# Row groups of the TensorE array for the target products of two layers of a graph network

## The chip, the cores and the metric

One core of one Trainium2 chip. The metric is the device time of one execution in microseconds, as a median over runs. TensorE is PE in the profile (its weight loads PEld), VectorE is DVE, ScalarE is ACT, GpSimd is POOL, and SP is the engine that issues most DMAs.

## What is computed

Four graph layers on 6250 nodes of 128 features and 100000 edges (`src`, `dst`, edge attributes, types and weights). Every layer sums something of the edges into nodes, goes through small dense layers and normalisations, and is added to x:

```
edge_index = jnp.stack([src, dst])
x = _layernorm(x + _L0_gnn_ref(x, edge_attr_128, ...))  # segment_sum(edge_attr, src) / count, then 3 x (linear, relu, batch norm)
x = _layernorm(x + _L1_gnn_ref(x, edge_index, ...))     # segment_sum(x[src], dst) / degree, + x, linear, relu
x = _layernorm(x + _L2_gnn_ref(x, edge_index, edge_type_3, ...))  # messages by edge type, segment_sum to dst, linear, norm, gelu
x = _layernorm(x + _L3_gnn_ref(x, edge_index, edge_weight, ...))  # segment_sum(x[src] * norm, dst), linear, relu, batch norm
```

The change concerns the sums into nodes of the first layer (layer 0: edge attributes by `src`) and of the last one (layer 3: weighted messages by `dst`).

## The kernel before, in words

Nodes are 49 groups of 128 (`GROUPS`). A first part (up to about 1110 us) sorts the edges into blocks of 4 (`BLK`) by groups of source and target node, and writes them as rows to the tables `slots` and `gbuf` in HBM. From then on everything goes by tiles: a tile is 128 blocks of 4 edges, 258 tiles (`TILES`) in 43 rounds (`RR`) of 6 (`RING`).

Each layer q has a target stage, `reduce(q)`, which sums the rows of a tile into a group of nodes. The same name stands once in PE's program and once in DVE's. For tile t, at place r = 0 to 5 of its round:

- SP loads the tile's rows, 128 partitions by 4 edges of 128 features and a few more values, into place r of a ring (`load_wide` for layers 0 and 1, with a second ring for the odd rounds; `load_tiles`, line 618 on, for layers 2 and 3, where the load waits until the products of the tile that held the place are made).
- A one-hot of the 4 x 128 target lanes is made in `hots[:, r, :]`: by DVE in one instruction (`one_hot`, line 1831), or for the places in `SCALAR_HOTS` by ACT in five (lines 936 and 940). ACT has place 5 in layer 0 and places 2 and 5 in layer 3, so DVE makes 5 and 4 one-hots a round. They are made for the round after: `one_hot(i + 1, r)` stands right behind the add of tile (i, r).
- PE (line 1379) waits for the one-hot, the rows, and the add of the tile three before, and makes 4 f32 products, one-hot by rows, which add up in PSUM bank r % 3. A product contracts over all 128 block rows and gives 128 nodes by `width` columns (129 in layer 0, 128 in layer 3). Each f32 product is two LDWEIGHTS and two MATMULs, here called two passes. The last one counts `products` up.
- DVE (line 1841) waits for `products` and for its own add before (`added`), and adds the bank to `sums` at a column that a register gives. The registers of a round's six tiles are loaded at the round's start by `loaded(at_sum, ...)` (line 501). `added` begins at 3.

In the code:

```
pe.wait_ge(added, t + (q * TILES + 1))
wait_rows(pe, q, i if h is None else h, r, odd)
for j in range(BLK):
    ins = pe.matmul(bank(r % 3, width), hots[:, r, j * P:(j + 1) * P], rows[:, j, 0:width],
                    start=j == 0, stop=j == BLK - 1)
ins.then_inc(products, 1)
```

POOL (`keep_lanes`) and ACT (`keep_pays`) take values out of the rows in layer 0. In layers 0 and 3 no other engine uses PSUM during the target stage; in layer 2 other products run beside it in banks 4 to 6. What comes after each target stage waits for its end.

Of the kernel before, what the change touches and what calls it, by code (L numbers as in the profile page):

```python
# [5 lines left out]
ALU = mybir.AluOpType  # L6
# [10 lines left out]
P = 128  # L17
# [30 lines left out]
BLK = 4  # L48
# [4 lines left out]
TILES = 258  # L53
RING = 6
# [24 lines left out]
RESTS = 5  # L79
PAIRS = 3  # L80
MSG_BANKS = 4
MIXED = 4 * STEP
GATHERED = {1: 0, 2: TILES, 3: 2 * TILES}

# [13 lines left out]
def fills_before(stage, r):  # L98
    def of(s):
        if s[0] == "g":  # L100
            return EVEN if s[1] < 2 else RR
        if s[1] == 2:
            return RR if r % LANE_SETS == 0 else 0
        return (EVEN, ODD, 0)[r % LANE_SETS]

    return sum(of(s) for s in FILLS[:FILLS.index(stage)])
# [74 lines left out]
def gnn_kernel(nc, x, src, dst, edge_attr, edge_type, edge_weight, u, W0, b0, W1, b1, W2, b2,  # L181
               g0, bt0, g1, bt1, g2, bt2, L1W, L1b, Wmsg, bmsg, Wupd, bupd, gam2, bet2,
               W3, b3, gam3, bet3, out):
    with ExitStack() as ctx:
# [3 lines left out]
        def sem(name):  # L188
            return ctx.enter_context(nc.semaphore(name))
# [90 lines left out]
        hots = hot_raw[:, :].rearrange("p (s n) -> p s n", s=RING)  # L280
# [91 lines left out]
        def bank(b, n=512):  # L372
            return ps[:, b, 0:n]
# [22 lines left out]
        tile_ready, tile_done, at_ready = sem("tile_ready"), sem("tile_done"), sem("at_ready")  # L396
# [5 lines left out]
        def odd_before(q, r):  # L402
            return (16 * ROUNDS if r < 3 else 0) + 16 * ODD * q

        def wait_rows(eng, q, h, r, odd):
            if odd:
                eng.wait_ge(odd_in[r], h * 16 + (odd_before(q, r) + 16))
            else:
                eng.wait_ge(rows_in[r], h * 16 + (16 * fills_before(("g", q), r) + 16))  # L410
        kept, hot_ready, products, added = sem("kept"), sem("hot_ready"), sem("products"), sem("added")
        far_ready, last_hots = sem("far_ready"), sem("last_hots")
        src_hots, gathered, staged = (sem(s) for s in ("src_hots", "gathered", "staged"))
        sent = [sem(f"sent{r}") for r in range(RING)]
        own_part, own_added = sem("own_part"), sem("own_added")
# [28 lines left out]
        def msg_bank(n):  # L444
            return bank(4 + n % MSG_BANKS, TYPES * D)

# [47 lines left out]
        def turned_keys(k):  # L494
            return ps[0:KROWS, 3 + k, 0:CB * P // 2].bitcast(BF16).rearrange("p (q n) -> p q n", q=CB)
# [373 lines left out]
        def _(act):  # L869
# [240 lines left out]
            def parts(i, operands=None):  # L1110
# [3 lines left out]
                for j in range(STEP):  # L1114
                    high_part(n + j)
                    if operands is not None:
                        g2_operand(operands, j)
                    if n < MIXED and j > 1:
                        mid_part(n + j - 2)
                if n < MIXED:  # L1120
                    for j in range(STEP - 2, STEP):
# [124 lines left out]
        def _(pe):  # L1246
# [14 lines left out]
            for k in range(2):  # L1261
                for q in range(CB):
                    ins = pe.transpose(turned_keys(k)[:, q, :], sg[:, k, q * KROWS:(q + 1) * KROWS], ident_h[:, :])
# [8 lines left out]
            for c in range(2):  # L1272
                ins = pe.matmul(ps[0:GROUPS, 7, 256:256 + GROUPS], ident[0:PAIR, c:PAIR:2], pair_sums[:, c:PAIR:2],
                                start=c == 0, stop=c == 1)
# [5 lines left out]
                      stop=True).then_inc(tables_turned, 1)  # L1280
# [50 lines left out]
            for k in range(2):  # L1331
                n = min(4, VECTORS - 4 * k) * D
                if k:
                    pe.wait_ge(prep_out, 6 + k)
                pe.matmul(bank(7, n), ones[0:1, :], bc_src[0:1, 4 * k * D:4 * k * D + n],
                          start=True, stop=True).then_inc(prep_t, 1)
# [20 lines left out]
            for k, b in ((0, 5), (1, 1)):  # L1357
                pe.matmul(bank(b, TILES), row128[0:GROUPS, 0:1].broadcast_to([GROUPS, P]), tile_on[:, k, :],
                          start=True, stop=True)
                pe.matmul(bank(b + 1, TILES), heads[:, 8 + k:9 + k].broadcast_to([GROUPS, P]), tile_on[:, k, :],  # L1360
                          start=True, stop=True)
                pe.matmul(bank(b + 2, TILES), ones[0:GROUPS, :], tile_on[:, k, :],
                          start=True, stop=True).then_inc(tile_done, 1)

            def reduce(q):
                width = ONE + 1 if q == 0 else AW if q == 1 else D

                def one_round(i, beside=False, h=None, odd=0):
                    for r in range(RING):
                        t = i * RING + r  # L1370
                        rows = rows_of(q, r, odd).rearrange("p (k w) -> p k w", k=BLK)
                        if r in VECTOR_HOTS[q]:
                            pe.wait_ge(hot_ready, hot_at(q, i, r))
                        else:
                            pe.wait_ge(last_hots, hot_at(q, i, r, SCALAR_HOTS))
                        pe.wait_ge(added, t + (q * TILES + 1))
                        wait_rows(pe, q, i if h is None else h, r, odd)
                        for j in range(BLK):
                            ins = pe.matmul(bank(r % 3, width), hots[:, r, j * P:(j + 1) * P], rows[:, j, 0:width],  # L1379
                                            start=j == 0, stop=j == BLK - 1)  # L1380
                        ins.then_inc(products, 1)
                        if beside and r == 0:
                            own_turn(i + 1)
                        if beside and r == RING // 2:
                            own_wide(i + 1)

                if q < 2:
                    with pe.Fori(0, ODD) as h:
                        for odd in range(2):
                            one_round(h * 2 + odd, h=h, odd=odd)  # L1390
                    one_round(RR - 1, h=ODD)
                    return
                if q == 2:
                    with pe.Fori(0, OWN_SETS) as i:
                        one_round(i, True)
                with pe.Fori(OWN_SETS if q == 2 else 0, RR) as i:
                    one_round(i)
# [93 lines left out]
            for k, stage in ((1, "mlp1"), (2, "mlp2")):  # L1491
                for n in range(2 * STEPS):
                    pe.wait_ge(bn_applied, (k - 1) * 2 * STEPS + n + 1)
                    pe.matmul(product_bank(stage, n), wT[:, 2 + k, :], A[:, n * HALF:(n + 1) * HALF],
                              start=True, stop=True).then_inc(st[stage]["m"], 1)
                if k == 1:
                    pe.wait_ge(lanes_ready, 3)
                    for v, table in enumerate((lanes, lanes_t)):
                        if v:
                            pe.wait_ge(lane_rows_made, v)  # L1500
                        for q in range(LTURNS):
                            ins = pe.transpose(lanes_turned[:, q, :], table[:, q * LCOLS:(q + 1) * LCOLS], ident_h[:, :])
# [28 lines left out]
            def g2_wide(i):  # L1531

                pe.wait_ge(st["g2"]["c"], i + 1)
                for j in range(STEP):
                    n = i * STEP + j
                    if n >= MSG_BANKS:
                        pe.wait_ge(st["g2"]["r"], n - MSG_BANKS + 1)
                    pe.matmul(msg_bank(n), zt2[:, j, :],
# [102 lines left out]
        def _(dve):  # L1641
# [48 lines left out]
            ins = ceil_shift(blocks_f[:, 0, :], small_i[0:GROUPS, :], ps[0:GROUPS, 7, 256:256 + GROUPS], BLK - 1, BLK_SHIFT)  # L1690
# [129 lines left out]

            def reduce(q, sums_from=None):
                width = ONE + 1 if q == 0 else AW if q == 1 else D
                k = 0 if q == 0 else 1

                def one_hot(i, r):
                    dve.wait_ge(products, i * RING + (q * TILES + r + 1))
                    if q < 2:
                        dve.wait_ge(kept, i * RING + (RING + q * TILES + r + 1))
                        dve.sem_inc(issued, 1)
                    lane = dst_lane[:, bass.ds(i * (RING * BLK) + r * BLK, BLK)][:, :, None]  # L1830
                    dve.tensor_tensor(hots[:, r, :].rearrange("p (k d) -> p k d", d=P),  # L1831
                                      lane.broadcast_to([P, BLK, P]),
                                      lane_ids[:, None, :].broadcast_to([P, BLK, P]), ALU.is_equal).then_inc(hot_ready, 1)

                def tiles(i, more=True):
                    at = loaded(at_sum, k, i, DVE, (GROUPS - 1) * AW)
                    for r in range(RING):
                        dve.wait_ge(products, i * RING + (q * TILES + RING + r + 1))
                        dve.wait_ge(added, i * RING + (q * TILES + r + 3))
                        to = sums_flat[:, bass.ds(at[r], width)]  # L1840
                        dve.tensor_tensor(to, to, bank(r % 3, width), ALU.add).then_inc(added, 1)  # L1841

                        if more and r in VECTOR_HOTS[q]:
                            one_hot(i + 1, r)

                for r in VECTOR_HOTS[q]:
                    one_hot(0, r)
                if sums_from is not None:
                    dve.wait_ge(*sums_from)

                with dve.Fori(0, RR - 1) as i:
                    tiles(i)
                tiles(RR - 1, False)
                dve.wait_ge(added, 3 + (q + 1) * TILES)
# [164 lines left out]
            for k, stage in enumerate(("mlp0", "mlp1")):  # L2019
                c, ins = batch_norm(k, stage, means_done if k == 0 else 0)  # L2020
                link(ins)
                for n in range(2 * STEPS):
                    t = A[:, n * HALF:(n + 1) * HALF]
# [61 lines left out]
            def g2_results(i, js=range(STEP)):  # L2085
                for j in js:
                    n = i * STEP + j
                    dve.wait_ge(high_ready, n + 1)
                    if n >= RESTS:
                        dve.wait_ge(low_ready, n - RESTS + 1)  # L2090
                    dve.tensor_tensor(rests[:, n % RESTS, :], msg_bank(n), part_of(0, n),
                                      ALU.subtract).then_inc(st["g2"]["r"], 1)
                    if n > MIXED:
                        mid_part(n - 1)

            def mid_part(n):
                dve.wait_ge(st["g2"]["r"], n + 1)
                if n == MIXED:
                    dve.wait_ge(mid_ready, MIXED)
                dve.tensor_copy(part_of(1, n), rests[:, n % RESTS, :]).then_inc(mid_ready, 1)  # L2100
# [90 lines left out]
            with dve.Fori(0, STEPS) as i:  # L2191
                for j in range(Z_CUT):
                    g = i * STEP + j
                    ins = dve.tensor_scalar(tile(At, g), tile(X, g), small[:, 0, bass.ds(g, 1)],
                                            small[:, 1, bass.ds(g, 1)], ALU.mult, ALU.add)
# [47 lines left out]
```

## Time and profile before

| | |
|---|---|
| median of 2 runs | 3754.14 us (3753.14 to 3755.14) |
| span of the profiled execution | 3754.1 us |
| target stage of layer 0 | 1110 to 1362 us |
| target stage of layer 3 | 3440 to 3692 us |
| PE, DVE, ACT, POOL busy over the span | 75%, 67%, 40%, 50% |

### The profile page before, as it was taken

How to read it: one execution, taken by the hardware profiler on the slowest of the kernel's cores; microseconds unless marked ns; L12 is line 12 of the kernel's file. 1: busy time of each engine (PE TensorE's matmuls, PEld its weight loads, DVE VectorE, ACT ScalarE, POOL GpSimd, SP SyncE). 2: the span in 40 equal slices, each digit the busy share in tenths (PEclk: the TensorE clock that was granted, in tenths of full speed). 3: DMA queues.
4: the chain of work that ended last, by engine and by line, in shares of the span. 5: the costliest groups of instructions: out<-in, count | busy, mean ns of one | idle time of the engine just before them, and what ended most of it. 6: DMA issues, size and time to landing. Idle time of an engine off the chain costs nothing.

```text
span 3754.1 us, 95326 instructions
## 1 busy us (share of the span) xinstructions
PE 2826.7 (75%) x23184; PEld 2448.4 (65%) x23185; DVE 2500.2 (67%) x7099; ACT 1518.9 (40%) x4337; POOL 1873.3 (50%) x2268
## 2 busy tenths in 40 slices
PE   8555544444439986778799799999999957777996
PEld 6232322222229965777799479999888957777995
DVE  7666666666647778555577777777666776554667
ACT  0111000000004445555576543222365347887665
POOL 4777777777763342777434344444432007774000
PEclk9999999999999998999899899999999969998998
DMA  6444444444449933888697035555477817786883
GB/s 214 151 149 144 146 149 141 149 143 147 148 130 290 291 128 118 279 275 277 221 290 255 9 127 180 173 183 177 136 226 235 263 38 269 275 275 197 286 281 122
DMA packets 419029, 721.55 MB, mean 192 GB/s; under 512 B 68624, under 2 KB 198169, under 8 KB 417932
## 3 DMA queue, kind: packets, MB, share of 16 engines
q1 hardware_dynamic: 330492, 494.35, 43.0%
q0 software_dynamic: 88464, 226.43, 16.0%
q14 instruction: 52, 0.43, 0.0%
q8 instruction: 21, 0.34, 0.0%
HBM read 481.26 MB, written 285.09 MB: 204 GB/s over the span
## 4 chain that ended last, share of the span: by engine, by line
PE 39%; POOL 23%; issue 14%; DMA 12%; DVE 5%; ACT 3%; SPq 2%; DVEq 1%; POOLq 1%; ACTq 0%
POOL slots L750 19%; PE ps L1379 18%; PE ps L1412 9%; DMA gbuf<-ring_raw,to_blk 8%; PE ps L1414 5%; POOL gbuf L804 4%; DMA ring_raw<-gbuf 3%; PE ps L1254 2%; PE ps L1465 1%; PE ps L1456 1%; SPq L501 1%; SPq L622 1%; DVE stats L1930 1%; PE ps L1521 1%; DVEq L501 1%
## 5 line engine op out<-in xcount | busy, mean ns | idle before, releaser
L804 POOL DMA_INDIRECT gbuf<-ring_raw,to_blk x774 | 754.2, 974 | 728.9 <-DVE ring_raw L1863 261.9
L750 POOL DMA_INDIRECT slots<-ring_raw,idx_edges x782 | 751.4, 961 | 242.3 <-issue 242.3
L1379 PE MATMUL ps<-ring_raw,memory 128*128 128x128 f32 (+2 forms) x6576 | 783.9, 279 | 84.9 <-DVE memory L1831 49.4
L1379 PEld LDWEIGHTS ps<-ring_raw,memory 128*128 128x128 f32 x6576 | 763.3, 192 | 113.1 <-issue 60.3
L1831 DVE TENSOR_TENSOR memory<-dst_lane,lane_ids 128x512 f32<-128x512 f32 x774 | 539.6, 698 | 73.3 <-POOL dst_lane L768 51.1
L1290 PE MATMUL ps<-memory 128*49 128x343 bf16 (+6 forms) x784 | 263.5, 489 | 387.9 <-DVE memory L1727 386.6
L1412 PE MATMUL ps<-memory 128*128 x2752 | 497.7, 273 | 10.2 <-DVE memory L1872 8.0
L1841 DVE TENSOR_TENSOR memory<-memory,ps 128x128 f32 (+2 forms) x1032 | 293.4, 284 | 314.7 <-PE ps L1379 302.6
L936 ACT ACTIVATE memory<-lane_ids,dst_lane 128x128 f32<-128x128 f32 x1032 | 331.0, 395 | 400.3 <-PE ps L1379 263.1
L1414 PE MATMUL ps<-memory 128*128 x2752 | 477.5, 220 | 0.0
L1290 PEld LDWEIGHTS ps<-memory 128*49 128x49 bf16 x784 | 113.9, 159 | 530.7 <-DVE memory L1727 301.9
L1424 PE MATMUL ps<-memory 128*128 x2064 | 270.2, 292 | 88.2 <-ACT ring_raw L977 49.9
L888 ACT COPY ring_raw<-memory 128x49 f32 (+1 forms) x112 | 26.0, 232 | 767.5 <-DMA slots<-ring_raw,idx_edges 767.4
L1424 PE MATMUL ps<-X,memory 128*128 x2064 | 267.0, 290 | 78.3 <-DVE memory L1886 31.0
L1424 PEld LDWEIGHTS ps<-memory 128*128 128x128 f32 x2064 | 255.8, 203 | 102.7 <-issue 101.3
L1424 PEld LDWEIGHTS ps<-X,memory 128*128 128x128 f32 x2064 | 252.8, 202 | 92.7 <-issue 91.8
L977 ACT ACTIVATE ring_raw<-ps,edge_w 128x128 f32<-128x128 f32 x1032 | 277.7, 407 | 68.9 <-issue 48.8
L1412 PEld LDWEIGHTS ps<-memory 128*128 128x128 bf16 x2752 | 269.8, 98 | 47.1 <-issue 15.2
L980 ACT COPY ring_raw<-ps 128x512 f32<-128x512 f32 x258 | 151.3, 586 | 361.9 <-PE ps L1414 361.9
L1863 DVE TENSOR_TENSOR ring_raw<-ring_raw,ps 128x512 f32<-128x512 f32 x258 | 177.5, 688 | 144.7 <-ACT ring_raw L980 144.7
L1414 PEld LDWEIGHTS ps<-memory 128*128 128x128 bf16 x2752 | 269.1, 98 | 2.4
L1886 DVE TENSOR_TENSOR memory<-memory,ps 128x512 f32<-128x512 bf16 x252 | 173.5, 689 | 112.4 <-PE ps L1424 112.4
(283 smaller groups left out, 4801.6 us busy)
## 6 DMA issues: line engine op xcount, KB each, us to landing
ring_raw<-gbuf SPq DMA_DIRECT2D x669, 268.0 KB, 3.7
ring_raw<-in_edge_attr SPq DMA_DIRECT2D x111, 448.0 KB
ring_raw<-slots SPq DMA_DIRECT2D x153, 272.0 KB, 4.0
zr<-lane_rows SPq DMA_DIRECT2D x87, 384.0 KB
zt<-lane_rows SPq DMA_DIRECT2D x87, 384.0 KB
memory<-lane_rows SPq DMA_DIRECT2D x84, 384.0 KB
memory<-slots SPq DMA_DIRECT2D x105, 272.0 KB, 4.0
memory<-gbuf SPq DMA_DIRECT2D x105, 268.0 KB, 3.8
```

The costliest lines, as they stand in the source:

```text
L750: pool.indirect_dma_start(edges, bass.IndirectOffsetOnAxis(idx_edges[0:n, u, j:j + 1], 0), edge_rows[0:n, u, j, :], None).then_inc(scatter ...
L804: pool.indirect_dma_start(gbuf, bass.IndirectOffsetOnAxis(to_blk[:, t:t + 1], 0), node_rows[:, r, :], None, bounds_check=NBLK - 1, oob_is_ ...
L936: ins = act.activation(hots[:, r, j * P:(j + 1) * P], lane_ids[:, :], ACT.Abs, bias=dst_lane[:, bass.ds(at, 1)], scale=-1.0)
L977: ins = act.activation(rows[:, j, 0:D], parts[:, j, :], ACT.Copy, scale=edge_w[:, bass.ds(at * BLK + j, 1)])
L1290: ins = pe.matmul(counts_of(s)[:, j * GROUPS:].rearrange("p (n g) -> p n g", g=GROUPS), hot2[:, u, 0, :, j], hot2[:, u, 1, :, j][:, None, ...
L1379: ins = pe.matmul(bank(r % 3, width), hots[:, r, j * P:(j + 1) * P], rows[:, j, 0:width], start=j == 0, stop=j == BLK - 1)
L1412: pe.matmul(to.rearrange("p (k d) -> p k d", d=D), hot, msgs[:, 0:2, bass.ds(at[r] + t * D, D)], start=t == 0, stop=False, skip_group_chec ...
L1414: ins = pe.matmul(to[:, D:2 * D], hot, msgs[:, 2, bass.ds(at[r] + t * D, D)], start=False, stop=t == TYPES - 1, skip_group_check=True)
L1424: ins = pe.matmul(bank(r)[:, j * P:(j + 1) * P], hots[:, r, j * P:(j + 1) * P], nodes[:, bass.ds(at[r], D)], start=True, stop=True)
L1831: dve.tensor_tensor(hots[:, r, :].rearrange("p (k d) -> p k d", d=P), lane.broadcast_to([P, BLK, P]), lane_ids[:, None, :].broadcast_to([P ...
L1841: dve.tensor_tensor(to, to, bank(r % 3, width), ALU.add).then_inc(added, 1)
L1863: dve.tensor_tensor(rows, rows, pair_bank(r)[:, :, 0:D], ALU.add).then_inc(staged, 1)
```

## The change

In layer 0 each product over 128 rows is made in 2 parts of 64 rows, in layer 3 in 4 parts of 32 rows. Each part uses its own group of rows of the array and adds up over the 4 edges of a block in a PSUM bank of its own, `r % turns + turns * v`. With 4 parts there are 2 sets of 4 banks (`turns` 2), otherwise 3 sets. PE waits for the add of the tile `turns` before. DVE adds the parts one after another to the same place, each waiting for the one before by the semaphore `part_added` (an alias of `tile_ready`, which was used once before, up to 1); the last add counts `added`. Layers 1 and 2 have one part, and with it the program of before.

```
+ROW_PARTS = (2, 1, 1, 4)
...
+        part_added = tile_ready
...
             def reduce(q):                                   # PE
                 width = ONE + 1 if q == 0 else AW if q == 1 else D
+                parts = ROW_PARTS[q]
+                turns = 2 if parts == 4 else 3
...
-                        pe.wait_ge(added, t + (q * TILES + 1))
+                        pe.wait_ge(added, t + (q * TILES + 4 - turns))
                         wait_rows(pe, q, i if h is None else h, r, odd)
+                        span = P // parts
                         for j in range(BLK):
-                            ins = pe.matmul(bank(r % 3, width), hots[:, r, j * P:(j + 1) * P], rows[:, j, 0:width],
-                                            start=j == 0, stop=j == BLK - 1)
+                            for v in range(parts):
+                                ins = pe.matmul(bank(r % turns + turns * v, width), hots[v * span:(v + 1) * span, r, j * P:(j + 1) * P],
+                                                rows[v * span:(v + 1) * span, j, 0:width], start=j == 0, stop=j == BLK - 1)
                         ins.then_inc(products, 1)
...
             def reduce(q, sums_from=None):                   # DVE
                 width = ONE + 1 if q == 0 else AW if q == 1 else D
+                parts = ROW_PARTS[q]
+                turns = 2 if parts == 4 else 3
+                part_base = 1 + sum(v - 1 for v in ROW_PARTS[:q]) * TILES
...
                         to = sums_flat[:, bass.ds(at[r], width)]
-                        dve.tensor_tensor(to, to, bank(r % 3, width), ALU.add).then_inc(added, 1)
+                        for v in range(parts - 1):
+                            dve.tensor_tensor(to, to, bank(r % turns + turns * v, width), ALU.add).then_inc(part_added, 1)
+                            dve.wait_ge(part_added, i * (RING * (parts - 1)) + (part_base + r * (parts - 1) + v + 1))
+                        dve.tensor_tensor(to, to, bank(r % turns + turns * (parts - 1), width), ALU.add).then_inc(added, 1)
```

## Rows read from the trace of the kernel before

**Rows 1.** The page: the chain that ended last, by line.

```profile
POOL slots L750 19%; PE ps L1379 18%; PE ps L1412 9%; DMA gbuf<-ring_raw,to_blk 8%; PE ps L1414 5%; POOL gbuf L804 4%; DMA ring_raw<-gbuf 3%; PE ps L1254 2%; PE ps L1465 1%; PE ps L1456 1%; SPq L501 1%; SPq L622 1%; DVE stats L1930 1%; PE ps L1521 1%; DVEq L501 1%
```

**Rows 2.** Windows, both stages: length, busy (x) of PE, PEld, DVE, ACT, POOL; PEclk, DMA.

```profile
1110.00:1362.00 252.00, 243.70 (x2064) 237.43 (x2064) 188.53 (x471) 116.49 (x473) 86.41 (x259) 1.00 0.88 282
3440.00:3692.00 252.00, 242.67 (x2064) 236.48 (x2064) 165.98 (x425) 168.30 (x420) 0.00 (x0) 0.99 0.88 280
```

**Rows 3.** Timeline of DVE in layer 0, two turns of a round: start, duration.

```profile
1249.82 0.29 DVE L1841 TENSOR_TENSOR memory<-memory,ps 128x129 f32 x1 [1.53 <-PE ps L1379]
1250.24 0.69 DVE L1831 TENSOR_TENSOR memory<-dst_lane,lane_ids 128x512 f32<-128x512 f32 x1
1250.86 0.28 DVE L1841 TENSOR_TENSOR memory<-memory,ps 128x129 f32 x1
...
1254.06 0.28 DVE L1841 TENSOR_TENSOR memory<-memory,ps 128x129 f32 x1
1255.28 0.29 DVE L1841 TENSOR_TENSOR memory<-memory,ps 128x129 f32 x1 [0.95 <-PE ps L1379]
...
1259.52 0.28 DVE L1841 TENSOR_TENSOR memory<-memory,ps 128x129 f32 x1
1261.33 0.29 DVE L1841 TENSOR_TENSOR memory<-memory,ps 128x129 f32 x1 [1.53 <-PE ps L1379]
```

**Rows 4.** Line 501 in layer 0's stage: register loads, ns min/median/max.

```profile
L501 DVEq TENSOR_LOAD <-at_sum x43: 811/1069/1427, 1114.3 to 1357.6; - x43
```

**Rows 5.** PE's waits, 1130 to 1350 and 3445 to 3690 us: total, times, longest.

```profile
PE ps L1379 <- DVE memory L1841: 6.5, 20, 0.6
...
PE ps L1379 <- DMA ring_raw<-gbuf: 8.2, 18, 1.0
```

**Rows 6.** Timeline of DVE in layer 3, two turns of a round.

```profile
3518.12 0.29 DVE L1841 TENSOR_TENSOR memory<-memory,ps 128x128 f32 x1
3519.66 0.29 DVE L1841 TENSOR_TENSOR memory<-memory,ps 128x128 f32 x1 [1.24 <-PE ps L1379]
...
3521.30 0.28 DVE L1841 TENSOR_TENSOR memory<-memory,ps 128x128 f32 x1
3521.78 0.29 DVE L1841 TENSOR_TENSOR memory<-memory,ps 128x128 f32 x1 [0.20 <-DVE memory L1841]
3522.00 0.69 DVE L1831 TENSOR_TENSOR memory<-dst_lane,lane_ids 128x512 f32<-128x512 f32 x1
...
3523.48 0.29 DVE L1841 TENSOR_TENSOR memory<-memory,ps 128x128 f32 x1
3525.62 0.29 DVE L1841 TENSOR_TENSOR memory<-memory,ps 128x128 f32 x1 [1.85 <-PE ps L1379]
```

**Rows 7.** Line 1841 over the span: ns min/median/max.

```profile
L1841 DVEq FUSED_REGOPS  x1032: 57/57/64, 1115.6 to 3692.3; - x172
L1841 DVE TENSOR_TENSOR memory<-memory,ps x1032: 271/284/296, 1115.7 to 3692.4; 128x128 f32 x86, 128x129 f32 x43, 128x133 f32 x43
```

**Rows 8.** Timeline of DVE in layer 1: two adds without a one-hot between.

```profile
1844.56 0.72 DVE L1841 TENSOR_TENSOR memory<-memory,ps 128x133 f32 x2
```

**Rows 9.** Timeline of DVE in a batch norm: chained one-column instructions.

```profile
1418.93 0.16 DVE L2015 TENSOR_TENSOR bn_c<-bn_c,cols 128x1 f32<-128x1 f32 x1
1419.12 0.16 DVE L2016 TENSOR_TENSOR bn_c<-bn_mv,bn_c 128x1 f32<-128x1 f32 x1
```

**Rows 10.** Timeline of PE: three tiles of layer 2; bf16 transposes.

```profile
2755.47 2.84 PE L1379 MATMUL ps<-ring_raw,memory 128*128 128x128 f32 x24
...
1415.90 0.83 PE L1502 MATMUL ps<-ident_h,edge_w 128*86 128x128 bf16 x12
```

**Rows 11.** Line 1379: weight loads and MATMULs, ns min/median/max.

```profile
L1379 PEld LDWEIGHTS ps<-ring_raw,memory x6576: 186/191/338, 1110.2 to 3691.9; 128*128 128x128 f32 x200
L1379 PE MATMUL ps<-ring_raw,memory x6576: 272/275/583, 1110.2 to 3692.0; 128*128 128x128 f32 x125, 128*128 128x129 f32 x38, 128*128 128x133 f32 x37
```

**Rows 12.** Window of the first part, columns as in rows 2.

```profile
300.00:900.00 600.00, 274.96 (x1878) 169.99 (x1879) 396.63 (x1631) 53.59 (x178) 455.40 (x474) 1.00 0.46 146
```

## Prediction

> **What bounds the kernel now.** The page comes first [rows 1]: the change touches the target stages of two layers alone, and their matmuls (line 1379, shared by four stages) are the largest PE entry in the chain that ended last. The windows by stage then tell the two touched stages apart [rows 2]: layer 0 runs from 1110 to 1362 us and layer 3 from 3440 to 3692 us, 252 us each, 504 of 3754. In both PE is busy 96 to 97%, DMA 88%, and DVE 66 to 75%. Each stage has 43 rounds of 6 tiles, so a round takes 5.86 us on average.
>
> A PE share near 97% reads as if PE alone were the bound; the timeline of DVE says otherwise [rows 3]. In layer 0 DVE adds a tile (0.28 us) and makes a one-hot (0.69 us) in turn. A one-hot is followed by the add 0.61 us later (1250.24 to 1250.86), and four such pairs take 3.20 us (1250.86 to 1254.06), 0.80 each, so that an add is followed by the one-hot 0.19 us later: no gap until 1254.34. Then it stands still until 1255.28, and a round later from 1259.80 to 1261.33. The row blames PE, but in those gaps DVE's queue loads the six addresses of the next round [rows 4] (0.8 or 1.4 us, once in each of the rounds). That it is DVE that is late can be seen on the other side: PE's only waits in this stage are for DVE's add, 6.5 us in all [rows 5]. So the DVE path is closed in layer 0: two rounds take 1261.33 - 1249.82 = 11.51 us, 5.755 each, and anything added to DVE lengthens them. In layer 3 the same loads stand at the turn of the round, DVE makes 4 one-hots a round in place of 5, and PE waits for rows too (8.2 us) [rows 5, 6]. There DVE has some room, PE and the row transfers next to none.
>
> **What the change adds on DVE.** Each tile's product now arrives in 2 banks (layer 0) or 4 (layer 3), and DVE adds them one by one into the same place, each waiting for the one before. That is 258 + 774 = 1032 more adds of 0.284 us: 293 us of busy work alone [rows 7], where DVE has 63 and 86 us idle in the two stages [rows 2]. Nothing hides this; layer 3 alone is over by 774 x 0.284 - 86 = 134 us.
>
> The real cost is the pitch of two dependent adds. The trace has such a pair wherever no one-hot stands between two tiles' adds: in layer 3 from 3521.30 to 3521.78, 0.48 us [rows 6], that is 0.28 of work, then the wait, an address instruction and the start. In layer 1 two adds last 0.72 us together, so the second starts 0.43 us behind the first [rows 8]. The small chained instructions of the batch norm have the least gap, 0.03 to 0.04 us behind an end, which would make 0.32 [rows 9]. I take 0.48, the row of this very stage, and keep 0.32 as the lower bound. As the upper one I add 0.10 (twice the 57 ns address instruction [rows 7], rounded) for a wait value that must be computed.
>
> Behind an add that had to wait, DVE's queue hasn't run ahead, and so the one-hot starts later: 0.42 us after the add in layer 0 (1249.82 to 1250.24) instead of 0.19 [rows 3], and 0.22 in layer 3 (3521.78 to 3522.00), where the one-hot has fewer waits [rows 6]. After the change every last add is of that kind.
>
> Layer 0, a round: five tiles with a one-hot at 0.48 + 0.42 + 0.61 = 1.51 us make 7.55; the sixth costs 0.48 and the turn of the round, from its last add to the next round's first, 1.22 or 1.81 us (1254.06 to 1255.28, 1259.52 to 1261.33), 1.515 on average. Sum 9.55 us against 5.755, so +3.79 us x 43 = **+163 us**.
>
> Layer 3, a round: 18 dependent steps at 0.48 make 8.64; four tiles with a one-hot at 0.22 + 0.61 make 3.32; the tile without one 0.48; the turn 1.54 or 2.14 (3518.12 to 3519.66, 3523.48 to 3525.62), mean 1.84. Sum 14.28 us against 5.86, so +8.42 us x 43 = **+362 us**.
>
> **What it does on PE.** A tile now takes 16 or 32 passes (LDWEIGHTS and MATMUL, two for each f32 product) where it took 8. A pass costs (2.84 - 0.275) / 23 = 0.112 us [rows 10], 0.275 us being one MATMUL's own duration. Two bounds. If passes of different row groups run side by side, a tile stays at 8 x 0.112 = 0.9 us. If matmuls start in order and the two passes of one product can't overlap, a product's second pass runs beside the next group's first: still 0.9 us in layer 0, and 16 x 0.112 = 1.8 us in layer 3. Issue isn't tighter: the bf16 transposes start (0.83 - 0.22) / 11 = 0.055 us apart [rows 10], 32 of them 1.8 us. All lie under DVE's 1.59 (9.55 / 6) and 2.38 us a tile, and cost nothing while DVE is that slow. The other end is no overlap at all, 1.79 and 3.58 us a tile; that is a rival below. I choose overlap because the groups use separate rows of the array, separate operands and separate banks, and because LDWEIGHTS and MATMUL already run together in these stages (237 and 244 us busy of 252) [rows 2].
>
> The Trainium skill, page TensorE: Matmul & The Clock Gate, Part 3, says that products in different row groups run concurrently, each in the time of a full one; no row of this trace has such products. By it PE would stay under DVE, as in the sum. The page TensorEngine Tiling (Array Packing), PSUM Bottleneck, warns that tiling speeds TensorE but not the evacuation of PSUM; it speaks against this change, and the evacuation here is DVE's adds [rows 7].
>
> Edits costed at nothing: in layer 3 only 2 sets of banks stand where 3 stood, so PE may be one tile ahead and not two. From the end of a tile's adds DVE needs 0.55 (the rest of its one-hot) + 1.44 + 0.83 = 2.8 us before it wants the product that PE may start then, and PE needs 1.8 + 0.3. The cover is gone if a tile takes PE over 2.8 us, and then it is the PE rival that holds. Layer 0 keeps 3 sets. SP's loads of rows, POOL's and ACT's work per tile stay the same and get more time: their queues wait for `products`, which comes later, and hide wholly behind DVE. Behind DVE's new waits stand the one-hots of the next round, which PE needs a full round later. Layers 1 and 2 have one part and are unchanged. The stages before and after are serial with these two and only shift.
>
> **The sum.** 163 + 362 = 525 us on the profiled execution's span of 3754.1 us, which equals the median of the timed runs (3754.14): **4279 us**, 14% slower.
>
> **Rivals.**
> - *PE becomes the bound.* No overlap between groups: 16 x 0.112 x 6 = 10.75 us a round in layer 0 (over DVE's 9.55) and 21.5 in layer 3 (over 14.28). That gives +215 and +673 us, **4642 us**. A clock at 1.2 GHz in layer 3 would do nearly the same, since doubled passes make 3.6 us a tile. For: a weight load lasts 191 ns beside a MATMUL's 275 [rows 11], so if loads queue one behind another across groups, 32 of them fill the tile's time. Against: separate rows, and the granted clock was 1.00 from 300 to 900 us with PE busy only 46% [rows 12]. It decides from 0.099 us a pass in layer 0 and 0.074 in layer 3.
> - *The dependent adds are cheap.* With 0.32 in place of 0.48 us: 24 steps x 0.16 x 43 = 165 us less, **4114 us**; with layer 1's 0.43, 4227. For: the chained small instructions. Against: both rows of this very instruction.
> - *Not slower.* VectorE isn't what sets the round: its part adds fit into its idle time, and PE or the rows go on setting 5.86 us. The price is 0, or a gain of at most what DMA's 88% share leaves, 0.12 x 504 = 60 us, **3694 to 3754 us**. It would need part adds of under 86 / 774 = 0.11 us in layer 3 where the trace has 0.284. So "faster by over 2%" (75 us) is nearly out of reach by any way.
> - *The change doesn't do what it says*: row groups that bring neither gain nor loss on PE are the forecast itself; the DVE adds are in the program in any case.
>
> **How the numbers follow.** Forecast (DVE sets both rounds at 0.43 to 0.58 us a step) 0.64, own range 4227 to 4382 (24 x 0.10 x 43 = 103 us above). PE the bound 0.24, around 4642. Cheap adds 0.09, 4114 to 4227. Not slower 0.03. To leave out no more than 2 in 10 the range has to take in the PE rival: 4110 to 4650. Slower by over 2% (about what a measurement of this kernel can tell from no change) 0.97, within 2% 0.02, faster 0.01.
>
> **What would show it.** Right: layer 0's target stage near 415 us and layer 3's near 615; DVE's start-to-start of two adds at 0.48 us, its waits for PE nearly gone; PE busy well under 90% in layer 0 and waiting for DVE's add; DMA share down to about 0.53 and 0.36. The PE rival: PE at 100% in layer 3, DVE waiting for PE, the stage near 925 us. Cheap adds: pitch of 0.32. The forecast is wrong if PE's passes there lie over 0.074 us apart on average, or if adds into one place don't wait for one another at the price seen.

## The result and the profile after

The changed kernel takes 4128.41 us (median of 2 runs, 4125.18 to 4131.63) against 3754.14: 1.0994 of the time before, 95% interval 1.0968 to 1.1021. The profiled execution has a span of 4123.4 us, 369.3 more than before. From the first to the last MATMUL of the target stages, layer 0 takes 376.0 us where it took 251.7, and layer 3 takes 495.6 where it took 251.4. That is +124 and +244 us, 368 of the 369; layers 1 and 2 are within 3 us of what they were.

The windows of the two stages in the changed kernel (length, busy time and count of PE, PEld, DVE, ACT, POOL, then PEclk and DMA; compare [rows 2]):

```profile
core 0: us, PE busy (x) PEld busy (x) DVE busy (x) ACT busy (x) POOL busy (x), PEclk, DMA share, GB/s
1110.00:1487.00 377.00, 300.71 (x4128) 252.31 (x4128) 278.27 (x729) 116.46 (x473) 90.62 (x261) 1.00 0.66 189
3563.00:4059.00 496.00, 343.85 (x8256) 302.46 (x8256) 385.36 (x1196) 168.21 (x420) 0.00 (x0) 0.88 0.52 142
```

PE has twice and four times the MATMULs, and is busy a smaller share of the time: 80% and 69%, after 97% and 96%. DVE went up to 74% and 78%, and what is missing there to 100% is no room, as its timeline shows. Layer 0, a round from first add to first add (compare [rows 3]; line 1851 adds a part, 1853 the last part, 1840 makes the one-hot):

```profile
1299.85 0.29 DVE L1851 TENSOR_TENSOR memory<-memory,ps 128x129 f32 x1 [1.82 <-PE ps L1385]
1300.17 0.29 DVE L1853 TENSOR_TENSOR memory<-memory,ps 128x129 f32 x1
1300.59 0.69 DVE L1840 TENSOR_TENSOR memory<-dst_lane,lane_ids 128x512 f32<-128x512 f32 x1
1301.20 0.28 DVE L1851 TENSOR_TENSOR memory<-memory,ps 128x129 f32 x1
1301.52 0.29 DVE L1853 TENSOR_TENSOR memory<-memory,ps 128x129 f32 x1
1301.91 0.69 DVE L1840 TENSOR_TENSOR memory<-dst_lane,lane_ids 128x512 f32<-128x512 f32 x1
...
1306.47 0.28 DVE L1851 TENSOR_TENSOR memory<-memory,ps 128x129 f32 x1
1306.78 0.29 DVE L1853 TENSOR_TENSOR memory<-memory,ps 128x129 f32 x1
1308.31 0.29 DVE L1851 TENSOR_TENSOR memory<-memory,ps 128x129 f32 x1 [1.23 <-PE ps L1385]
...
1317.36 0.29 DVE L1851 TENSOR_TENSOR memory<-memory,ps 128x129 f32 x1 [1.82 <-PE ps L1385]
```

Part add to last add is 0.32 us, last add to one-hot 0.39 to 0.42, one-hot to the next tile's add 0.61, and the turn of the round, where the queue loads its registers, 1.53 (1306.78 to 1308.31) or 2.11 us. Two rounds take 1317.36 - 1299.85 = 17.51 us, 8.755 each, and 43 of them 376 us: the whole stage. (The gap of 2.11 us lies between an add of 1315.25, not shown, and that of 1317.36.) In layer 3 (compare [rows 6]) three part adds stand in one row:

```profile
3805.20 0.69 DVE L1840 TENSOR_TENSOR memory<-dst_lane,lane_ids 128x512 f32<-128x512 f32 x1
3805.81 0.92 DVE L1851 TENSOR_TENSOR memory<-memory,ps 128x128 f32 x3
3806.77 0.29 DVE L1853 TENSOR_TENSOR memory<-memory,ps 128x128 f32 x1
3808.30 0.94 DVE L1851 TENSOR_TENSOR memory<-memory,ps 128x128 f32 x3 [1.24 <-issue]
3809.26 0.29 DVE L1853 TENSOR_TENSOR memory<-memory,ps 128x128 f32 x1
3809.49 0.69 DVE L1840 TENSOR_TENSOR memory<-dst_lane,lane_ids 128x512 f32<-128x512 f32 x1
```

From the first part add to the last add are 0.96 us, 0.32 a step (3805.81 to 3806.77). And PE in layer 3, first one tile with its 32 passes, then four tiles in one row:

```profile
3803.63 1.11 PE L1385 MATMUL ps<-ring_raw,memory 32*128 32x128 f32 x32
...
3637.22 6.94 PE L1385 MATMUL ps<-ring_raw,memory 32*128 32x128 f32 x128 [0.49 <-DVE memory L1853]
```

The first row is one tile, 32 passes in 1.11 us. Less the 0.27 us of one MATMUL, 0.84 us: the passes start in fours, and seven steps between the eight fours make 0.12 us each. One by one, at the 0.112 of [rows 10], they would last 3.6 us. The row groups do run side by side, all four of them. The second row is made mostly at another clock, four tiles in 6.94 us. The clock granted in layer 3 changed between its two levels (1.00 is 2.4 GHz, 0.50 is 1.2) in stretches of 3 to 21 us, which makes the 0.88 above. Two windows, one at either level:

```profile
3626.00:3636.00 10.00, 5.95 (x172) 5.01 (x168) 7.51 (x25) 3.28 (x8) 0.00 (x0) 1.00 0.59 164
3636.60:3643.20 6.60, 6.11 (x108) 5.83 (x108) 5.63 (x18) 2.00 (x5) 0.00 (x0) 0.50 0.42 122
```

At the lower level a tile takes up to 2.1 us in this trace. DVE's rounds last 11.57 us on average, 1.93 a tile, so DVE can come to wait for PE there. The two places of DVE's timeline are the same step of a round (last add of place 2 to first add of place 3, with no one-hot between):

```profile
3627.01 0.29 DVE L1853 TENSOR_TENSOR memory<-memory,ps 128x128 f32 x1
3627.45 0.94 DVE L1851 TENSOR_TENSOR memory<-memory,ps 128x128 f32 x3
...
3638.66 0.29 DVE L1853 TENSOR_TENSOR memory<-memory,ps 128x128 f32 x1
3639.57 0.94 DVE L1851 TENSOR_TENSOR memory<-memory,ps 128x128 f32 x3 [0.63 <-PE ps L1385]
```

It takes 0.43 us in the 15 rounds of 43 in which PE made place 3's product at full clock, and 0.77 on average in the other 28. PE for its part waits for DVE's last add, where before it waited 6.5 us for DVE's add in layer 0 and 8.2 us for rows in layer 3 [rows 5]; its waits from 1130 to 1450 us and from 3590 to 4040 us:

```profile
PE ps L1385 <- DVE memory L1853: 62.1, 182, 1.3
...
PE ps L1385 <- DVE memory L1853: 137.9, 178, 1.9
```

Last, the two lines of the adds over the whole span (compare [rows 7]), to which the text comes back:

```profile
L1851 DVE TENSOR_TENSOR memory<-memory,ps x1032: 275/286/292, 1115.6 to 4059.8; 128x128 f32 x129, 128x129 f32 x43
L1851 DVEq FUSED_REGOPS  x516: 57/57/64, 1115.5 to 4059.1; - x172
...
L1853 DVE TENSOR_TENSOR memory<-memory,ps x1032: 272/289/296, 1116.0 to 4060.2; 128x128 f32 x86, 128x129 f32 x43, 128x133 f32 x43
L1853 DVEq FUSED_REGOPS  x516: 57/57/64, 1945.7 to 3127.1; - x172
```

### The profile page after: what moved, and what is told of

It reads as the page before. It is cut to its first block, busy times and chain, and to the rows that moved or that the text cites. A ratio compares the mean times of both kernels' runs of the same rounds, so it can differ in the third digit from the quotient of the medians.

```text
span 4123.4 us, 113668 instructions
## 1 busy us (share of the span) xinstructions
PE 2981.2 (72%) x31440; PEld 2523.4 (61%) x31441; DVE 2810.4 (68%) x8131; ACT 1519.1 (37%) x4337; POOL 1871.8 (45%) x2268
## 4 chain that ended last, share of the span: by engine, by line
PE 33%; POOL 21%; issue 17%; DVE 11%; DMA 9%; DVEq 4%; ACT 3%; SPq 1%; POOLq 1%; ACTq 0%
POOL slots L752 18%; PE ps L1385 14%; PE ps L1418 8%; DMA gbuf<-ring_raw,to_blk 7%; DVE memory L1851 6%; PE ps L1420 4%; POOL gbuf L806 3%; DVEq L503 2%; DVE memory L1853 2%; PE ps L1256 1%; PE ps L1471 1%; PE ps L1462 1%; DMA ring_raw<-gbuf 1%; ACT ring_raw L979 1%; DVE stats L1942 1%
## 5 line engine op out<-in xcount | busy, mean ns | idle before, releaser
L1385 PE MATMUL ps<-ring_raw,memory 32*128 32x128 f32 (+3 forms) x13992 | 922.7, 303 | 262.3 <-DVE memory L1853 186.0
L1385 PEld LDWEIGHTS ps<-ring_raw,memory 32*128 32x128 f32 (+2 forms) x13992 | 839.0, 207 | 355.4 <-issue 212.5
L1851 DVE TENSOR_TENSOR memory<-memory,ps 128x128 f32 (+1 forms) x1032 | 295.0, 286 | 183.3 <-PE ps L1385 133.3
```

The lines of the kernel that those rows point to most:

```text
L1385: ins = pe.matmul(bank(r % turns + turns * v, width), hots[v * span:(v + 1) * span, r, j * P:(j + 1) * P], rows[v * span:(v + 1) * span, j ...
L1851: dve.tensor_tensor(to, to, bank(r % turns + turns * v, width), ALU.add).then_inc(part_added, 1)
```

## The experiments

The questions were whether DVE's adds are the whole loss or PE's half has a part in it, why a dependent add costs 0.32 us and not 0.48, and whether anything else in the design is worth its price. Times are medians beside runs of the kernel before on the same chip; "stage" is from the first to the last MATMUL of a target stage.

**PE's half alone.** The row groups and banks stay, DVE adds only the last part.

```
-                        for v in range(parts - 1):
-                            dve.tensor_tensor(to, to, bank(r % turns + turns * v, width), ALU.add).then_inc(part_added, 1)
-                            dve.wait_ge(part_added, ...)
```

> PE's half alone: the products are made in row groups and in banks of their own as in the changed kernel, but VectorE adds only the last part of each tile. It leaves out the sums of the other parts (three quarters of layer 3's rows, half of layer 0's). VectorE theory (the adds are the whole loss, row groups run side by side): near the kernel before, 3754 us, at most 20 to 40 us more in layer 3 because two sets of banks stand where three stood and VectorE's stop of 1.5 to 2.1 us at the turn of a round reaches PE sooner. PE theory (short passes, a granted clock of 0.88 and two sets of banks cost much of it): over 3850 us.

3775.85 us, 1.0051 of the kernel before (1.0034 to 1.0068). Layer 0's stage is 251.0 us with twice the MATMULs, nothing lost and nothing gained. Layer 3's, with four times the MATMULs and two sets of banks, is 271.2, 20 more:

```profile
1112.00:1363.00 251.00, 243.50 (x4126) 237.54 (x4128) 189.05 (x471) 116.47 (x473) 93.03 (x258) 1.00 0.88 283
3438.00:3709.00 271.00, 250.17 (x8245) 240.74 (x8249) 169.73 (x425) 168.25 (x420) 0.00 (x0) 0.99 0.84 260
```

With DVE's adds gone, PE in layer 0 is as busy as in [rows 2], 97% at the same clock. In layer 3 it is busy 92% where it was 96%, but its 250 us of busy time are close to the 243 of before. So 4 passes of 32 rows take about the time of one of 128. Where the 20 us come from is the question of two more runs below.

**DVE's half alone.** PE as before, DVE adds the one bank 2 or 4 times.

```
-                            for v in range(parts):
-                                ins = pe.matmul(bank(r % turns + turns * v, width), hots[v * span:(v + 1) * span, ...
+                            ins = pe.matmul(bank(r % 3, width), hots[:, r, j * P:(j + 1) * P], rows[:, j, 0:width], ...
...
-                            dve.tensor_tensor(to, to, bank(r % turns + turns * v, width), ALU.add)...
+                            dve.tensor_tensor(to, to, bank(r % 3, width), ALU.add)...
```

> VectorE's half alone: PE makes whole products in three banks as before, VectorE adds the one bank 2 times (layer 0) or 4 times (layer 3) with the waits of the changed kernel. The sums are too large by these factors. VectorE theory: as slow as the changed kernel, 4110 to 4135 us, layer 0's target stage 376 us and layer 3's 490 to 500 us. PE theory: under 4050 us.

4121.85 us, 1.0966 (1.0947 to 1.0984). Layer 0's stage is 376.7 us (376.0 in the full change) and layer 3's 482.5 (495.6), 8 under the expected 490. With no row group anywhere the loss is there: 125 of 124 us in layer 0 and 231 of 244 in layer 3. The granted clock in layer 3 fell here too, to 0.89, with PE busy 69% as in the full change; so the short passes aren't needed for it. With three sets of banks it cost nothing: the step from place 2 to place 3 is 0.43 to 0.44 us on average at either level of the clock.

```profile
1112.00:1488.00 376.00, 299.35 (x2060) 251.08 (x2061) 276.94 (x726) 116.47 (x473) 87.49 (x260) 1.00 0.65 189
3572.00:4054.00 482.00, 331.72 (x2061) 291.05 (x2062) 382.48 (x1191) 168.20 (x420) 0.00 (x0) 0.89 0.52 146
```

**Two sets of banks, whole products.** The kernel before, with `bank(r % 2)` in layer 3 and PE waiting for the add of the tile two before.

```
-                        pe.wait_ge(added, t + (q * TILES + 1))
+                        pe.wait_ge(added, t + (q * TILES + (2 if q == 3 else 1)))
...
-    bank(r % 3, width)
+    bank(r % (2 if q == 3 else 3), width)
```

> The kernel before with 2 PSUM banks in place of 3 in layer 3's target stage (PE waits for the add of the tile two before), whole products, no row groups. Set theory (the 20 us that PE's half alone cost in layer 3 come from the missing third set: VectorE's stop at the turn of a round reaches PE): layer 3's stage 270 us where it had 251, 3774 us. Row-group theory (quarter passes themselves cost it): stage 251 us, 3755 us.

3774.24 us, 1.0041 (1.0027 to 1.0055), stage of layer 3 269.3 us. The same 18 to 20 us as in PE's half alone, without any row group. In a stage that PE bounds the third set was worth this much: it carried PE over DVE's stop at the turn. PE now waits once in nearly every round, before the product of place 2, for the first add after the turn (waits from 3450 to 3700 us):

```profile
PE ps L1379 <- DVE memory L1841: 24.4, 40, 0.9
```

**Row groups with three sets in both layers.** PE's half alone, with ROW_PARTS (2, 1, 1, 2).

> PE's half alone with ROW_PARTS (2, 1, 1, 2): row groups in both layers, 3 sets of banks in both, VectorE adds only the last part of each tile (the sums of the other half are left out). Set theory: both stages at 251 us, 3755 us: row groups neither cost nor give anything. Row-group theory: layer 3's stage between 251 and 270 us.

3755.77 us, 0.9995 (0.9985 to 1.0005); stages 251.2 and 250.5 us. With three sets, 2 row groups are worth nothing in either direction; with two sets, 4 row groups and whole products differ by 2 us (271.2 and 269.3). The 20 us of PE's half belong to the set.

**Layer 0 alone**, ROW_PARTS (2, 1, 1, 1).

> ROW_PARTS (2, 1, 1, 1): layer 0 alone in parts. If the two stages are independent, layer 0's stage grows by 124 us as in the full change and the time is 3878 us. If the first stage's part owes something to the other, it differs by more than 10 us.

3884.94 us, 1.0339 (1.0322 to 1.0357); stages 375.6 and 248.0 us. 7 us over the expected time, with layer 0's stage as expected; the kernel before had 3757.41 in these runs, 3 above its first median. The rest of the difference lies outside layer 0's stage, in stretches that differ by 2 to 6 us from run to run; layer 3's stage, which the edit leaves as it was, is 3 us shorter. By no more than that do the two stages act on each other.

**Layer 3 alone in 2 parts**, ROW_PARTS (1, 1, 1, 2).

> ROW_PARTS (1, 1, 1, 2): layer 3 alone, in 2 parts with 3 sets of banks. VectorE theory by the steps of the changed kernel's trace (dependent add 0.32, add to one-hot 0.205, one-hot to add 0.61, add to the next tile's add 0.43, turn 1.82 us): a round of 4 x 1.135 + 0.75 + 2.14 = 7.43 us against 5.86, so +67 us, 3821 us. If two sets of banks or the quarter passes were what costs in layer 3, this version would be near 3754 us.

3831.28 us, 1.0196 (1.0179 to 1.0213); layer 3's stage is 318.9 us, +67.5, where the steps of the trace gave +67. The whole time is 10 us over the expected 3821, of which 3 are the kernel before in these runs (3757.41); the rest lies outside this stage. The sum by steps works for the stage once the step has its right size.

**An address for each part add.** Each part goes to the place of another tile of the round.

```
-                        to = sums_flat[:, bass.ds(at[r], width)]
+                        to = sums_flat[:, bass.ds(at[(r + parts - 1) % RING], width)]
...
-                            dve.tensor_tensor(to, to, bank(r % turns + turns * v, width), ALU.add).then_inc(part_added, 1)
+                            part_to = sums_flat[:, bass.ds(at[(r + v) % RING], width)]
+                            dve.tensor_tensor(part_to, part_to, bank(r % turns + turns * v, width), ALU.add).then_inc(part_added, 1)
```

> The changed kernel, but each part of a tile is added to the place of another tile of the round (registers at[(r + v) % 6]), so that every add needs an address instruction of its own between its wait and its start. Parts other than the intended ones land in other groups of nodes, so the sums are wrong. Address theory (0.48 us in layer 3 of the kernel before was 0.32 plus the address instruction; the changed kernel reuses the address): a step goes from 0.32 to 0.43 to 0.48 us, 24 steps x 0.11 to 0.16 x 43 = +113 to +165 us on the changed kernel's 4128, 4241 to 4293 us. Rival (the longer pitch before came from the two waits, products and added, and not from the address): 4120 to 4135 us.

4173.01 us, 1.1111 (1.1094 to 1.1128). Slower than the changed kernel by 45 us, which is under the 113 expected at least, and over the rival's 4135 us. The edit put address instructions onto the dependent steps only in some places. Layer 0 (lines 1852 part, 1854 last):

```profile
1300.30 0.28 DVE L1852 TENSOR_TENSOR memory<-memory,ps 128x129 f32 x1
1300.62 0.29 DVE L1854 TENSOR_TENSOR memory<-memory,ps 128x129 f32 x1
...
1303.60 0.28 DVE L1852 TENSOR_TENSOR memory<-memory,ps 128x129 f32 x1
1304.03 0.29 DVE L1854 TENSOR_TENSOR memory<-memory,ps 128x129 f32 x1
...
L1852 DVEq FUSED_REGOPS  x172: 57/57/64, 1114.9 to 4098.4; - x172
...
L1854 DVEq FUSED_REGOPS  x860: 57/57/64, 1115.4 to 4102.3; - x172
```

In layer 0 five of six tiles have 0.43 us between the adds, the sixth 0.32. In layer 3, in each of the 43 rounds, all three steps of place 0 are 0.43 and the last step of places 1 and 2; the other thirteen are 0.32, as their addresses had been made for a tile before. That is 5 long steps a round in either layer, where 24 in all were expected. Over the span there are 172 + 860 = 1032 address instructions, as many as the 516 + 516 of the changed kernel. But 344 more of them (860 - 516) now stand at line 1854 between a wait and the last add, and 86 of the 172 of line 1852 (two a round in layer 3) between a wait and a part add: 430, ten a round. Where one stands there the step is 0.11 us longer. Layer 0's stage grew by 400.8 - 376.0 = 24.8 us, and 5 steps x 0.11 x 43 are 24. Layer 3's grew by 18.0 us, less than these 24. The theory holds in kind and size a step; how many steps the edit would lengthen was misjudged.

**One-hots moved to ScalarE**, in the changed kernel.

```
-SCALAR_HOTS = ((5,), (2, 5), (5,), (2, 5))
+SCALAR_HOTS = ((2, 5), (2, 5), (5,), (0, 2, 3, 5))
```

> The changed kernel with SCALAR_HOTS (2, 5) in layer 0 and (0, 2, 3, 5) in layer 3: one and two one-hots a round go from VectorE to ScalarE, nothing else changes. VectorE theory: a moved one-hot takes 0.39 + 0.61 - 0.5 = 0.5 us a round off VectorE's path in layer 0 and 0.205 + 0.61 - 0.43 = 0.385 us each in layer 3, so -21 and -33 us, 4074 us. If something else sets the round (PE with its colder clock, rows), the time stays at 4128 us; ScalarE has 4 x 1.95 = 7.8 us of one-hots in a round of 11.5, and would be seen as the releaser if it were late.

4075.33 us, 1.0845 (1.0828 to 1.0861), against 4074 expected. Stages 352.2 and 468.5 us, 24 and 27 less than in the changed kernel, where 21 and 33 were expected. DVE's path is the bound there: what leaves it leaves the time.

**The same in layer 0 of the kernel before**, SCALAR_HOTS[0] = (2, 5).

> The kernel before with the one-hot of place 2 in layer 0 made by ScalarE. If VectorE's path is closed in layer 0 (11.51 us for two rounds, where PE's passes take 96 x 0.112 = 10.75 and its own waits are 6.5 us in the stage), this gives up to 6.5 us: 3748 to 3752 us. If PE and the rows set the round and VectorE is only close to them: 3754 us, or more where ScalarE's one-hot comes late.

3753.89 us, 0.9998 (0.9989 to 1.0007); layer 0's stage 250.8 us, 251.7 before. No gain. But the run doesn't decide between its two theories, since DVE's path wasn't shortened by the edit:

```profile
1250.48 0.28 DVE L1841 TENSOR_TENSOR memory<-memory,ps 128x129 f32 x1
1250.68 0.69 DVE L1831 TENSOR_TENSOR memory<-dst_lane,lane_ids 128x512 f32<-128x512 f32 x1
1251.28 0.72 DVE L1841 TENSOR_TENSOR memory<-memory,ps 128x129 f32 x2
1252.11 0.69 DVE L1831 TENSOR_TENSOR memory<-dst_lane,lane_ids 128x512 f32<-128x512 f32 x1
1252.72 0.28 DVE L1841 TENSOR_TENSOR memory<-memory,ps 128x129 f32 x1
1253.10 0.69 DVE L1831 TENSOR_TENSOR memory<-dst_lane,lane_ids 128x512 f32<-128x512 f32 x1
1253.71 0.28 DVE L1841 TENSOR_TENSOR memory<-memory,ps 128x129 f32 x1
```

From the add of place 1 to that of place 5 are 3.23 us (1250.48 to 1253.71), and 3.20 with the one-hot on DVE [rows 3]. The moved one-hot took 0.4 us off, since the adds of places 2 and 3 now stand 0.43 us apart. But the next two one-hots start 0.40 and 0.38 us behind the starts of their adds where they had started 0.20 behind (on average of the stage they are 0.27 and 0.09 later). The queue gets to the first only when the dependent add before it has been started; the second had to wait in this round for the lanes that POOL makes for it. PE's waits for DVE's add are 6.5 us as before. Whether PE or the rows would have set the round next stays open.

**All four parts in one reduction** in layer 3 of the changed kernel, with the parts of a tile in neighbouring banks.

```
+                        if parts == 4:
+                            part_sum = zr[:, r % 2, :]
+                            dve.tensor_reduce(part_sum, ps[:, 4 * (r % 2):4 * (r % 2) + 4, 0:D].rearrange("p v n -> p n v"), AX_X,
+                                              ALU.add).then_inc(part_added, 1)
+                            dve.wait_ge(part_added, i * RING + (part_base + r + 1))
+                            dve.tensor_tensor(to, to, part_sum, ALU.add).then_inc(added, 1)
```

> The changed kernel, but in layer 3 VectorE sums the 4 parts with one reduction over 4 neighbouring banks (128 x 512 elements read, into SBUF) and adds the result in a second instruction; the result is the same sum in another order. VectorE theory: 0.69 us, as a one-hot of 512 elements, and some 0.04 us to the add, against 3 x 0.32 = 0.97: 0.24 us less a tile, -62 us, about 4065 us. If the chain of dependent adds isn't what sets layer 3, no change from 4128 us.

4087.95 us, 1.0881 (1.0863 to 1.0899), stage of layer 3 450.7 us, 45 less than in the changed kernel where 62 were expected.

```profile
3801.80 0.68 DVE L1852 TENSOR_REDUCE zr<-ps 128x128 f32<-128x512 f32 x1
3802.62 0.29 DVE L1855 TENSOR_TENSOR memory<-memory,zr 128x128 f32 x1
3803.08 0.69 DVE L1852 TENSOR_REDUCE zr<-ps 128x128 f32<-128x512 f32 x1 [0.16 <-PE ps L1385]
3803.91 0.29 DVE L1855 TENSOR_TENSOR memory<-memory,zr 128x128 f32 x1
```

The reduction costs the expected 0.68 us, but the add starts 0.14 us behind its end and not 0.04: its address, which the reduction doesn't share, is made in between, the same 0.11 us as above. And DVE begins to wait for PE (0.16 us in the third row), which two sets of banks keep at most a tile ahead; the granted clock was 0.50 there (3802 to 3804 us), and at full clock this wait is not seen in the stage.

No version with all its sums beat the kernel before, and the runs say why: the row groups give PE nothing, so that every added instruction on DVE is pure price.

## Why the prediction was right, and where it was not

The direction was right and for the reason given: DVE's added work sets both stages, and the adds alone bring nearly the whole loss. The price was forecast at 525 us and is 374. The range of 4110 to 4650 us holds the 4128, but only 18 us from its lower end; the forecast's own range, 4227 to 4382, doesn't. The wide range had been stretched over the rivals, and that the cheap adds, with 0.09 the least likely of those that cost time, lay just inside it was luck.

**What bounds the stages** was right where it mattered: DVE's path in layer 0 was closed, and everything added to it lengthened the rounds (8.755 us for 5.755). In the trace of the kernel before, the products of that stage had ended a median of 1.1 us before their adds began. That PE or the rows stand close behind DVE there isn't shown by any run, nor is the opposite: the one run made for it left DVE's path as long as it was.

**PE's side** was right at its favourable end. Four groups ran side by side, and the two passes of one f32 product were no worse than before: 1.11 us a tile where the PE rival had 3.6. The rule of the Trainium skill, page TensorE: Matmul & The Clock Gate, Part 3, that products in different row groups run concurrently agrees with the row of 32 passes in 1.11 us. The rule of the Trainium skill, page TensorEngine Tiling (Array Packing), PSUM Bottleneck, that the evacuation doesn't get faster, is the result of the whole case: DVE's half alone makes 1.0966 of 1.0994.

**The dependent step** is what failed, the term "24 steps at 0.48 us". It measured 0.317 us in layer 0 and 0.321 in layer 3, the price of the rival *the dependent adds are cheap* (0.32), whose 4114 us is 14 us from the result where the forecast's 4279 is 151 away. The cause is one instruction in DVE's queue. The pair I took from [rows 6] adds two different tiles, so between the wait and the add the queue makes the second one's address. The parts of one tile share the address: line 1851 has 516 address instructions, one a tile, and line 1853 has none outside layers 1 and 2. With the address put back the step was 0.43, the figure of [rows 8]. The last 0.05 us up to 0.48 were a wait for PE: in 40 of the 43 such pairs of layer 3 in the kernel before, the second add starts 0.14 to 0.23 us behind the end of PE's product, and the pairs are 0.43 to 1.77 us long; in the three where the product had ended at least 0.27 us before, they are 0.42 to 0.43. The row that I took showed PE's pace and only happened to lie near DVE's. Both rows were of "this very instruction", as the prediction said, and still of another situation; the rows of the chained small instructions [rows 9], of another instruction in the same situation, had the right gap.

The sizes: layer 0 was put at +163 and gave +124. Six steps 0.163 shorter are 42 us less, the one-hot 0.02 to 0.03 earlier some 5 less, but the turn 1.82 instead of 1.515 is 13 more (the queue starts to load the registers 0.38 us behind the start of the last add, where it was 0.10, in a round of each trace). The last 4 are an error of the sum: it takes 43 x 5.755 = 247.5 us as the stage of before, which is 251.7 us long.

Layer 3 was put at +362 and gave +244. 18 steps 0.159 shorter are 123 us less, and the rest is 5 more. The tile without a one-hot was put at 0.48 to the next and took 0.65 on average (7 us more), for a reason that the prediction didn't have. DVE's half alone accounts for 231 of the 244. The other 13 come with the missing third set, which the prediction had at nothing, and the lower clock together. With two sets, DVE's steps to the next tile are longer only where PE made the product wholly or partly at the lower level; added up this is 12 us. With three sets and the same clock (DVE's half alone) they aren't. The cover that the prediction counted, 2.8 us against PE's 2.1, was smaller with the cheaper steps: before place 3, where no one-hot comes first, it is 0.52 + 0.96 + 0.43 = 1.9 us. PE needs 1.2 + 0.3 at full clock and 2.1 + 0.3 at the lower level. In the kernel before the same set is worth 18 to 20.

**The clock** fell to 0.88 in layer 3, which I had held unlikely by the window of the first part [rows 12]. PE stood idle there for 31% of the stage, a little at each tile; in layer 0, where it stood idle for 20%, the clock stayed at 1.00. The fall came in DVE's half alone just as much, and cost nothing there. In the full change it is the other condition of the 12 us above.

## What to carry to other kernels

Splitting a full contraction into row groups gave TensorE nothing here, because the groups together do the work of one full pass in the time of one; it only multiplies the banks that someone has to add. Before splitting, count what the adding engine gets per tile against its idle time: 774 adds of 0.28 us against 86 us idle decided this case, whatever the details. When a pitch between dependent instructions is taken from a trace, first see whether the second of them waited for something else, and then look at what the queue does between the wait and the start (an address from a register, a computed wait value) and whether the new instruction needs it too.

## What the runs showed of the hardware that I had not expected

- All four row groups of 32 rows overlap for f32 products: 32 pairs of LDWEIGHTS and MATMUL in 1.11 us, where one by one at 0.112 us they would need 3.6. So the weight loads of different groups don't queue one behind another either.
- An address instruction between a wait and its add costs 0.11 us a step (0.32 to 0.43), twice its own 57 ns, and it isn't counted as busy time.
- Where DVE is the bound, a set of banks fewer and a lower clock can cost together what neither costs alone: inside the rounds of layer 3 of the changed kernel DVE waited for PE only at products made wholly or partly at the lower level (up to 2.1 us a tile), and with a third set not at all. Where PE is the bound the set has its price at full clock as well (18 us).
- Four times the MATMUL instructions cost PE next to nothing: with DVE's part adds left out and two sets of banks, layer 3's 8256 passes took 271.2 us, and 2064 whole ones with two sets took 269.3.
